# One core's attention and fp8 linear: the last key's p v products of eight-key tiles on ScalarE, and another division of the last two tiles

## What is computed

```python
xn = _layernorm(x)
qkv = xn @ Wqkv.T + bqkv                  # 16 heads of 32
scores = mask + scale * einsum('bnd,bmd->bnm', q, k)
out = einsum('bnm,bmd->bnd', softmax(scores), v)
attn = out @ Wproj.T + bproj
ffn = (fp8(xn) @ fp8(weight).T).astype(f32) + bias
x = x + attn + ffn
```

## Time and profile before

| What | us |
|---|---|
| median of three runs | 1536.07 |
| the profiled execution | 1536.16 |
| its span, first to last instruction | 1534.4 |
| TensorE busy in it | 1505.7 (98%) |
| DVE busy | 1446.9 (94%) |
| POOL busy | 1354.8 (88%) |
| ACT busy | 1038.6 (68%) |

### The profile page before, as it was taken

How to read it: one execution, slowest core, us unless ns; L and a number is a source line. 1 busy time by engine, 2 the same in 40 slices (tenths; PEclk the granted TensorE clock), 3 DMA queues, 4 the chain that set the end, 5 groups by cost and what they waited for, 6 DMA issues and landing times. The chain is left out here.

```text
span 1534.4 us, 23337 instructions
## 1 busy us (share of the span) xinstructions
PE 1505.7 (98%) x7022; PEld 692.4 (45%) x7022; DVE 1446.9 (94%) x1220; ACT 1038.6 (68%) x2000; POOL 1354.8 (88%) x1026
## 2 busy tenths in 40 slices
PE   6999999999999999999999999999999999999997
PEld 3444444444444444444444444444444444444455
DVE  6999999999999999999999999999999999999995
ACT  5676766767766767666767666776666767667642
POOL 2579999999899989999999899989999999899983
PEclk9999999999999999999999999999999999999999
DMA  7444554545445455554545455554554545455332
GB/s 225 89 100 104 132 117 110 135 110 130 119 113 124 117 130 115 127 119 113 132 110 136 115 115 128 114 130 108 129 119 113 130 115 135 112 115 125 94 104 62
DMA packets 362350, 182.98 MB, mean 119 GB/s; under 512 B 310000, under 2 KB 310000, under 8 KB 362224
## 3 DMA queue, kind: packets, MB, share of 16 engines
q1 hardware_dynamic: 362224, 181.49, 49.6%
HBM read 73.41 MB, written 33.55 MB: 70 GB/s over the span
## 5 line engine op out<-in xcount | busy, mean ns | idle before, releaser
L550 POOL TENSOR_TENSOR prod_pv<-kv,probs 128x2048 f32<-128x2048 f32 x182 | 662.8, 3642 | 9.5
L1156 DVE TENSOR_REDUCE scores<-prod_qk 128x64 f32<-128x2048 f32 x192 | 439.3, 2288 | 6.8 <-DVE prod_qk L1151 0.2
L1244 DVE TENSOR_REDUCE o_nat<-prod_pv 128x512 f32<-128x2048 f32 (+1 forms) x121 | 404.6, 3344 | 40.9 <-POOL prod_pv L550 23.4
L1151 DVE TENSOR_TENSOR prod_qk<-q_ps,kv 128x1536 f32<-128x1536 f32 (+1 forms) x192 | 397.9, 2073 | 0.2 <-issue 0.2
L909 PE MATMUL k_ps<-wqkv_hi,xT 128*128 128x512 f16 x1024 | 326.2, 380 | 3.8 <-DMA xT<-x 3.2
L909 PE MATMUL v_ps<-wqkv_hi,xT 128*128 128x512 f16 x1024 | 325.5, 379 | 0.0
L909 PE MATMUL q_ps<-wqkv_hi,xT 128*128 128x512 f16 x1024 | 325.5, 379 | 0.0
L909 PE MATMUL proj_ps<-wproj_hi,oT 128*128 128x512 f16 x952 | 302.6, 379 | 0.0
L759 ACT ACTIVATE kv<-v_ps 128x512 f32<-128x512 f32 x128 | 142.2, 1111 | 150.7 <-PE v_ps L909 150.7
L909 PE MATMUL k_ps<-wqkv_lo,xT 128*128 128x512 f16 x512 | 194.4, 380 | 0.0
L909 PE MATMUL q_ps<-wqkv_lo,xT 128*128 128x512 f16 x512 | 194.1, 379 | 0.0
(11 more groups left out here) (173 smaller groups left out, 1981.9 us busy)
## 6 DMA issues: line engine op xcount, KB each, us to landing
xn<-in_L_attn_x SPq DMA_DIRECT2D x132, 256.0 KB, 2.9
xs<-in_L_attn_x SPq DMA_DIRECT2D x124, 256.0 KB, 2.6
out<-xs SPq DMA_DIRECT2D x124, 256.0 KB, 2.1
xT<-x SPq DMA_TRANSPOSE x256, 3.0
kv<-in_L_attn_Wqkv SPq DMA_DIRECT2D x3, 1024.0 KB, 8.1
oT<-o SPq DMA_TRANSPOSE x122, 3.2
kv<-in_L_attn_Wproj SPq DMA_DIRECT2D x1, 1024.0 KB, 6.1
prod_pv<-in_L_ffn_weight SPq DMA_DIRECT2D x1, 1024.0 KB, 9.8
```

What stands on the lines that cost most here:

```text
L550: nc.gpsimd.tensor_tensor(o, v, p, ALU.mult).then_inc(pv_multiplied, 1)
L1151: nc.vector.tensor_tensor(prod_qk[:, 1:1 + m0 + 4 - m1, :], qb, k, ALU.mult).then_inc(qk_multiplied, 1)
L1156: nc.vector.tensor_reduce(scores[:, n % 2, :, m0:m0 + 4].rearrange("p h m -> p m h"), prod_qk[:, row:row + 4, :].rearrange("p m (h d) -> p ...
L1244: nc.vector.tensor_reduce(o_nat[:, n % 2, :], prod_pv[:, place:place + units, :].rearrange("p q (c m) -> p c q m", m=4), AX_XY, ALU.add).t ...
```

## The change

In the slots, the second unit of a heavy tile on POOL covers three keys instead of four. ScalarE makes the fourth one's products (key 7) in 16 instructions of 32 numbers, one per head, each scaled by the head's probability (a number per partition): eight of them stand before line 748 and eight behind line 655. A new semaphore, last_key_multiplied, tells POOL (before it overwrites the probabilities) and DVE (before line 1244) when they are done. The 60 heavy tiles up to the ninth from the end are concerned.

In the ending, tile t - 2 leaves SUMMED: DVE sums its two units, ScalarE and DVE split it, and SP turns it by a DMA transpose. POOL makes both units of tile t - 1, so DVE makes the second unit only of t - 3 and t - 2. The order at the end is t - 3, t - 4, t - 1, t - 2 instead of t - 3, t - 2, t - 4, t - 1. DVE does late_sum(t - 6) and late_sum(t - 5) between the new steps. In the diff sum_keys and low_half_of_o hold what lines 1313 to 1318 and 1322 to 1324 did for t - 4, now also for t - 2.

```diff
-SUMMED = (TILES - 7, TILES - 6, TILES - 5, TILES - 3, TILES - 2, TILES - 1)
-SHARED = TILES - 3
-IN_TURN = (TILES - 9, TILES - 8, TILES - 7, TILES - 6, TILES - 5, TILES - 3, TILES - 2, TILES - 4, TILES - 1)
+SUMMED = (TILES - 7, TILES - 6, TILES - 5, TILES - 3, TILES - 1)
+SHARED = (TILES - 3, TILES - 2)
+IN_TURN = (TILES - 9, TILES - 8, TILES - 7, TILES - 6, TILES - 5, TILES - 3, TILES - 4, TILES - 1, TILES - 2)
...
@@ SP, ending @@
-                turn_o(TILES - 4, 1, late_o_lo_ready)
-                for t in IN_TURN[3:]:
+                turn_o(TILES - 4, 1, late_o_lo_ready, turn(TILES - 6))
+                store(TILES - 6)
+                turn_o(TILES - 2, 2, late_o_lo_ready, turn(TILES - 6))
+                for t in IN_TURN[4:]:
                     store(t)
...
@@ POOL, products @@
+                if m0:
+                    v, p, o = v[:, :, :, 0:3], p[:, :, :, 0:3], o[:, :, :, 0:3]
...
@@ POOL, ending @@
                 t = TILES - 1
-                pool.wait_ge(pv_multiplied, units_before(TILES - 3) + 1)
-                probabilities(0, t, PROMPT)
+                probabilities(0, t, N)
                 late_products(t, 0)
+                late_products(t, 1)
...
@@ ACT, slots @@
+            def last_key_products(i, n, first, last):
+                u = key_units(n)[1][0]
+                after(act, probs_ready, tile_count(i, n))
+                after(act, v_kept, tile_count(i, N * (n // N) + N - 1))
+                after(act, pv_summed, unit_count(i, u - PRODS))
+                for h in range(first, last):
+                    step = nc.scalar.activation(prod_pv[:, u % PRODS, :].rearrange("p (c m) -> p c m", m=4)[:, h * D:(h + 1) * D, 3],
+                                                v_all[:, (n // N) % 2, h * D:(h + 1) * D, N - 1], ACT.Copy,
+                                                scale=probs[:, n % 2, h, N - 1:N])
+                if last == H:
+                    step.then_inc(last_key_multiplied, 1)
...
+                if live(i, j, L_PV) and keys_of(j - L_PV) == N:
+                    last_key_products(i, j - L_PV, 0, H // 2)
                 if live(i, j, L_KV):
                     n = j - L_KV
...
                     preset_k()
+                if live(i, j, L_PV) and keys_of(j - L_PV) == N:
+                    last_key_products(i, j - L_PV, H // 2, H)
...
@@ ACT, ending @@
-                split_o(t - 4, units_before(t - 7) + 2)
+                round_linear(t - 4)
                 low_of_turned(t - 3)
-                round_linear(t - 2)
-                preset_late(t - 2)
-                high_of_turned(t - 2)
-                low_of_turned(t - 2)
-                round_linear(t - 4)
+                split_o(t - 4, units_before(t - 7) + 2, t // OT - 3)
                 preset_late(t - 4)
                 high_of_turned(t - 1)
                 round_linear(t - 1)
+                low_of_turned(t - 1)
                 preset_late(t - 1)
-                low_of_turned(t - 1)
+                split_o(t - 2, units_before(t - 7) + 4, t // OT - 4)
+                round_linear(t - 2)
+                preset_late(t - 2)
...
@@ PE, ending @@
                 late_linear(t - 3)
                 sum_unit(t - 3, 0)
                 sum_unit(t - 3, 1)
+                late_linear(t - 4)
                 rest(t - 3)
+                late_projection(t - 3)
+                sum_unit(t - 1, 0)
+                sum_unit(t - 1, 1)
+                late_linear(t - 1)
+                rest(t - 1)
+                late_projection(t - 4)
                 late_linear(t - 2)
-                late_projection(t - 3)
-                sum_unit(t - 2, 0)
-                sum_unit(t - 2, 1)
-                rest(t - 2)
-                late_linear(t - 4)
-                sum_unit(t - 1, 0)
+                late_projection(t - 1)
                 late_projection(t - 2)
-                sum_unit(t - 1, 1)
-                rest(t - 1)
-                late_linear(t - 1)
-                late_projection(t - 4)
-                late_projection(t - 1)
...
@@ DVE, slots @@
+                    if units == 2:
+                        after(dve, last_key_multiplied, heavy_count(i, n))
...
@@ DVE, ending @@
+                sum_keys(TILES - 4)
                 late_sum(TILES - 7)
                 second_probabilities(TILES - 2)
                 second_products(TILES - 2)
-                dve.wait_ge(o_hi_ready, TILES - 6)
-                nc.vector.tensor_tensor(o16[:, t % 2, C:2 * C], o_nat[:, t % 2, :], o16[:, t % 2, 0:C],
-                                        ALU.subtract).then_inc(late_o_lo_ready, 1)
-                second_probabilities(TILES - 1)
-                second_products(TILES - 1)
-                for t in IN_TURN[3:]:
+                low_half_of_o(TILES - 4)
+                late_sum(TILES - 6)
+                sum_keys(TILES - 2)
+                late_sum(TILES - 5)
+                low_half_of_o(TILES - 2)
+                for t in IN_TURN[5:]:
                     late_sum(t)
```

More of the change, by code:

```diff
@@ L99, in late_turn, with tile @@
     return IN_TURN.index(t)
+def tile(i, n):
+    return i * PAIR + n
 def summed_turn(t):
@@ L287, in attention_and_fp8_linear @@
         pv_multiplied = sem("pv_multiplied")
+        last_key_multiplied = sem("last_key_multiplied")
         pv_summed = sem("pv_summed")
@@ L307, in late_oT, with late_half @@
         def late_oT(t):
-            return xT[:, t % XT, :, :] if t in SUMMED else oT[:, t % OT, :, :]
+            return xT[:, t % XT, :, :] if t in SUMMED or t == TILES - 2 else oT[:, t % OT, :, :]
+        def late_half(t):
+            return (1 if t == TILES - 2 else t) % 2
         def late_xs(t):
@@ L320, in second_p @@
         def second_p(t):
-            at = 4 * H * (t - SHARED)
+            at = 4 * H * SHARED.index(t)
             return q_ps[3][:, at:at + 4 * H].rearrange("p (h m) -> p h m", m=4)
@@ L511, in probabilities @@
                 after(pool, inv_ready, tile_count(i, n))
-                after(pool, pv_multiplied, unit_count(i, last_unit(n - 2)))
+                if tile(i, n) == TILES - 1:
+                    pool.wait_ge(pv_multiplied, units_before(n - 2) + 1)
+                else:
+                    after(pool, pv_multiplied, unit_count(i, last_unit(n - 2)))
+                after(pool, last_key_multiplied, min(heavy_count(i, n - 2), heavy_count(0, TILES - N - 1)))
                 nc.gpsimd.tensor_tensor(probs[:, n % 2, :, 0:keys], exps[:, n % 4, :, 0:keys],
@@ L771, in copy_query, with split_o @@
                 nc.scalar.activation(q_first[:, :], q_ps[t % 4][:, :], ACT.Copy).then_inc(q_copied, 1)
-            def split_o(t, summed):
+            def split_o(t, summed, turned):
+                h = late_half(t)
                 act.wait_ge(pv_summed, summed)
-                act.wait_ge(oT_moved[t % OT], 16 * (t // OT) if t < SUMMED[0] else 16 * (t // OT - 1))
-                nc.scalar.activation(o16[:, t % 2, 0:C], o_nat[:, t % 2, :], ACT.Copy).then_inc(o_hi_ready, 1)
+                act.wait_ge(oT_moved[h], 16 * turned)
+                nc.scalar.activation(o16[:, h, 0:C], o_nat[:, h, :], ACT.Copy).then_inc(o_hi_ready, 1)
             def scale_projected(t):
@@ L988, in sum_unit @@
             def sum_unit(t, q):
-                if q == 1:
-                    pe.wait_ge(late_pv_multiplied, t - SHARED + 1)
-                else:
-                    pe.wait_ge(pv_multiplied, units_before(min(t, SHARED)) + max(t - SHARED, 0) + 1)
+                if q == 1 and t in SHARED:
+                    pe.wait_ge(late_pv_multiplied, SHARED.index(t) + 1)
+                else:
+                    pe.wait_ge(pv_multiplied, units_before(t) + q + 1 - sum(s < t for s in SHARED))
+                if q == 0:
                     if summed_turn(t) > 2:
@@ L1291, in late_sum, with sum_keys, low_half_of_o @@
                                                in1=late_xs(t), op0=ALU.mult, op1=ALU.add).then_inc(late_y_ready, 1)
+            def sum_keys(t):
+                if t in SHARED:
+                    dve.wait_ge(late_pv_multiplied, SHARED.index(t) + 1)
+                    dve.wait_ge(pv_multiplied, units_before(t))
+                else:
+                    dve.wait_ge(pv_multiplied, units_before(t + 1))
+                    dve.wait_ge(o_lo_ready, TILES - 7)
+                both = (prod_pv[:, units_before(t) % PRODS:units_before(t) % PRODS + 2, :] if t not in SHARED else
+                        kv[:, 2 * N * C:2 * N * C + 2 * QUAD].rearrange("p (q x) -> p q x", q=2))
+                nc.vector.tensor_reduce(o_nat[:, late_half(t), :], both.rearrange("p q (c m) -> p c q m", m=4),
+                                        AX_XY, ALU.add).then_inc(pv_summed, 2)
+            def low_half_of_o(t):
+                h = late_half(t)
+                dve.wait_ge(o_hi_ready, {TILES - 4: TILES - 6, TILES - 2: TILES - 5}[t])
+                nc.vector.tensor_tensor(o16[:, h, C:2 * C], o_nat[:, h, :], o16[:, h, 0:C],
```

(9 more changed lines are left out.)

15 lines of the change are left out of this document (8 added, 7 removed).

## The result

The changed kernel takes 1526.71 us, the median of four runs (1525.74 to 1527.35), beside 1536.17 for the kernel before (1536.03 to 1536.29) on the same chip: a ratio of 0.9937, 95% interval 0.9925 to 0.995. It is faster by 9.5 us, and 1525.1 was predicted. The profiled execution took 1526.15, its span is 1524.4, 10.0 shorter than before.

What follows compares the result with a forecast made beforehand. TensorE was taken to bound the slots, DVE the ending until 1503.3, then TensorE. Gains 2.5 + 2.9 + 5.6 = 11.0 us from 1536.16 gave 1525.2, by the runs' median 1525.1; range 1521.0 to 1534.5.

Steps and rivals of the forecast that it cites:

- Part 1, ScalarE's c: Heavy slots, ScalarE's 16 instructions: each takes c = 0.24 us start to start, ends 0.17 and 0.31.
- The lateness: ACT in the slots: 2.5 us late after four heavy slots, caught up in the four light ones.
- Cost on the path: nothing: Slots: ScalarE's added instructions cost the path nothing, up to c = 0.294 us.
- a slack of 6.1 us: Ahead of the transposed x: ACT's fp8 half has 6.1 us spare before TensorE's k waits.
- Part 2: Slots, POOL's second unit with three keys: 2.85 us, 0.79 less; 2.5 us gained, ends 0 and 4.6.
- about half: Slots: 2.5 of the 4.6 us TensorE lost there would come back.
- Part 3, the lead: DVE's sum of tile 119 starts 2.9 us earlier, bounded by ACT's second eight; ends 0 and 3.7.
- Part 4, the ending: Last tiles: the new order saves 5.6 us, ends 4 and 6, TensorE losing 32 transposes of t - 2.
- the pause of 1511.9: Ending: TensorE pauses until 1512.8, perhaps lowering its clock, +0.85 us, half of it counted.
- The third rival: Ending: DVE's sum, ScalarE's split and the transpose land after 1522.3; with 3 us, 1528; chance 0.12.

Runs made afterwards that it cites:

- experiment 8: ScalarE's 16 products of key 7 and the waits for them left out, POOL keeping three keys, against experiment 1's kernel: 1518.73 us.
- experiment 4: Slots of the changed kernel with the ending of the kernel before: 1527.57 us, ratio 0.9943 to the kernel before.
- experiment 7: Four of ScalarE's second-half products made twice in every heavy slot (20 small instructions for 16), against experiment 1's kernel: 1540.91 us.
- experiment 5: All keys of tile 119 multiplied on POOL again, ScalarE keeping its products in the other heavy tiles, against experiment 1's kernel: 1521.30 us.
- experiment 1: DVE's small probabilities instruction of t - 2 moved ahead of POOL's two products of t - 1, against the changed kernel: 1522.51 us.
- experiment 2: Small probabilities instruction of t - 2 left in place but reading the reciprocals from PSUM, against the changed kernel: 1522.34 us.
- experiment 3: New ending alone, POOL making all four keys and ScalarE none, against the changed kernel: 1535.99 us, ratio 0.9997 to the kernel before.

## Why the prediction was right, and where it was not

The direction and the time (1525.1 against 1526.7, inside 1521.0 to 1534.5) held, but two terms were off by 3 and 4 us in opposite directions. That the sum came within 1.6 us is luck: with the ending as it turned out and the other terms as predicted it would have been 1529.4.

- **Part 1, ScalarE's c.** Right: 0.244 us against 0.24, so two strided sides cost what the row of one strided write priced for both. ACT busy is 1258.5 us, 1269 was given. (The 1036 us from which the prediction's 1269 starts is a slip for 1038.6.) The lateness was 1.1, not 2.5, for two reasons. The slot's idle stretches in the earlier trace rows are printed from the end of the previous instruction, while ACT's instructions start 0.1 us or more before their predecessor's end where nothing holds them (1409.05 after 1408.17 + 1.09), so the three stretches together held about 0.3 us more, and the later slots added nothing. And in the first heavy slot ACT no longer waited 1.62 us for DVE, but 0.66 and 0.18 for TensorE's projection and linear. "Cost on the path: nothing" holds for the slots (experiments 8 and 4). It does not for the whole: experiment 8 shows that ScalarE's part costs 3.8 us, and that DVE starts the ending 4.9 us later with it. The cover of that "nothing", a slack of 6.1 us, was wrong as well. It was read off one chain, ACT's fp8 half to TensorE's k. In experiment 7 TensorE was already losing time while that chain still had 2.8 us to spare, since DVE and POOL were late and made ACT later in turn (3.6 us after the first slot). Counted as the expectation of experiment 7 counts, the loss began at a lateness of 1.1 + 2.7 = 3.8. The turning point came out nearly right by luck, since the smaller lateness and the smaller room cancel: 2.7 to 3.1 us over 64 instructions is 0.042 to 0.048 more each, c = 0.286 to 0.292, where 0.294 stood.
- **Part 2.** POOL's unit: right, 0.85 against 0.79. Its effect was too low: of the loss of 4.6 in the slots "about half" was taken, and all of it came back, with 0.8 more from ahead of 183.88. That is +3.0 on the term. It is POOL's unit that does it: experiment 8 has the same 11.44 us with no products on ScalarE.
- **Part 3, the lead.** Right, and by the mechanism named: 3.2 against 2.9, ended by ACT's second eight (2.00 us of wait at 1442.79; experiment 5).
- **Part 4, the ending.** This is the step that failed: 1.35 in place of 5.6. The working put DVE's second product of t - 2 at 1509.3, beside POOL's products of t - 1 from 1505.5 to 1512.8, in times of before. Moved by 8.7, DVE reached it at 1500.5, as laid out. But the small instruction ahead of it, which no sentence of the prediction names, was costed at what it took while POOL stood idle, 0.23 us at 1509.27 in the trace of before, although the prediction's own times have POOL at work from 1505.5 to 1512.8. Beside POOL it takes 3.45 (experiments 1 and 2). The transpose of o for t - 4 was issued at 1506.9 instead of 1503.7. TensorE waited 2.54 us for it, and came out of that at the lower of its two clocks: eight matmuls in 3.43 us, 0.43 each instead of 0.216, with a granted clock of 0.54 from 1510 to 1513, where 0.50 is its level of 1.2 GHz. That is another 1.7 us. Together 4.2 us, as much as is missing (5.6 - 1.35). The prediction had allowed for such a loss of clock, at the pause of 1511.9 and by half. That pause came too, 1.27 us ahead of 1503.95, and there the granted clock stayed at 1.00 until 1508. The third rival, a late serial chain, is what happened, one link earlier than it stood there: at the transpose of t - 4, not of t - 2. Experiment 1 takes the collision away and has 5.1 us from the ending.

## What to carry to other kernels

When an instruction is moved, cost it beside its new neighbours on the other engines too. VectorE's instructions that read two SBUF tensors are the ones to look at, if GpSimd is in a long one; another place or one operand in PSUM takes the wait away. And when work is handed to an engine with idle time, ask which engine then waits for it and how much idle time that one has: here, in the slots of the changed kernel, ScalarE had 13 us of 95 left and VectorE 3, and with four more instructions a slot TensorE lost time behind VectorE and GpSimd before ScalarE's own chain had used up its room.

## What the runs showed of the hardware

- A VectorE instruction with two operands in SBUF and only 64 numbers a partition took 3.45 us (3.44 in experiment 3) instead of 0.23, until the GpSimd product that was running had ended (1503.99 against 1503.89); with one operand in PSUM it took 0.22 at the same place. The price is the rest of GpSimd's instruction, not a share of speed: 1.74 and 1.37 us for the low half of o instead of 0.68, and in both cases its end came 0.5 us after that of GpSimd's product (1504.90 after 1504.35, 1504.54 after 1504.00).
- ScalarE's instruction of 32 numbers with a read stride of 32 bytes and a write stride of 16 followed its like at 0.244 us, the mean of eight in a row.
- GpSimd's product with an inner run of three instead of four numbers costs nearly as much per number: 2793 / 1536 = 1.82 ns against 3643 / 2048 = 1.78.
